# Retention layer: two of four pair sums of the absolute products move to accumulating DMAs, and PE sums four groups per phase

## The reference

```python
xf = _gn(x).reshape(B, L, E)                       # B 8, L 1024, E 256
q, k, vr = xf @ Wq.T, xf @ Wk.T * SCALING, xf @ Wv.T   # 8 heads of 32
qr, kr = theta_shift(q, sin, cos), theta_shift(k, sin, cos)
qk = einsum('bhqd,bhkd->bhqk', qr, kr) * mask
den = clip(abs(qk).sum(-1, keepdims=True), 1.0, 50000.0)
qk = qk / den
out = einsum('bhqk,bhkd->bhqd', qk, vr)
out = layernorm(out) * ln_g + ln_b                 # over the 32 of a head
x = x + gelu(out) @ Wo.T
```

## Time and profile before

| what | value |
|---|---|
| median of 3 runs | 2510.02 us (2508.24 to 2511.22) |
| profiled execution | 2510.04 us, its span 2508.2 us |
| PE busy | 2455.6 us, 98% |
| DVE busy | 1838.1 us, 73% |
| ACT busy | 1475.6 us, 59% |
| POOL busy | 885.2 us, 35% |
| retention layer, 31 of its 32 phases | 954.71 us |

### The profile page before, as it was taken

One profiled execution on the slowest core, in us unless ns is written; L12 is line 12 of the kernel. 1 busy time (PEld: TensorE's weight loads), 2 busy tenths in 40 slices (PEclk: granted clock), 3 DMA queues, 4 the chain that ended last, 5 costly groups with the idle time before them and its releaser, 6 DMA issues. The chain is left out here.

```text
span 2508.2 us, 39426 instructions
## 1 busy us (share of the span) xinstructions
PE 2455.6 (98%) x14854; PEld 1765.2 (70%) x14854; DVE 1838.1 (73%) x2789; ACT 1475.6 (59%) x2077; POOL 885.2 (35%) x627
## 2 busy tenths in 40 slices
PE   8999999999999999999999699999999999999999
PEld 4444444444444444799999588888888888888888
DVE  5888888888888888777776586666666666666665
ACT  3676666676767676566566365555555555555554
POOL 3787777777777777212112100000000000000000
PEclk9999999999999999999999899999999999999999
DMA  7232323232323233123232340000000000000000
GB/s 248 50 79 66 87 68 87 67 88 68 88 67 89 65 90 82 60 81 122 68 108 78 96 152 26 26 26 26 26 25 18 26 26 26 26 19 16 26 18 17
DMA packets 116972, 158.48 MB, mean 63 GB/s; under 512 B 16160, under 2 KB 82216, under 8 KB 116528
## 3 DMA queue, kind: packets, MB, share of 16 engines
q1 hardware_dynamic: 116256, 155.25, 21.0%
q10 hardware_dynamic: 528, 0.72, 0.1%
HBM read 71.99 MB, written 33.59 MB: 42 GB/s over the span
## 5 line engine op out<-in xcount | busy, mean ns | idle before, releaser
L579 DVE TENSOR_TENSOR l_prod<-scores,l_window 128x1024 f32<-128x1024 f32 x512 | 613.4, 1217 | 140.7 <-PE scores L438 132.7
L792 ACT ACTIVATE l_absp<-l_prod 128x1024 f32<-128x1024 f32 x512 | 540.1, 1056 | 294.9 <-DVE l_prod L579 285.0
L1887 ACT ACTIVATE e_r<-e_h,e_bn,e_rs 128x512 f32<-128x512 f32 x512 | 399.2, 780 | 484.6 <-PE e_h L1738 479.1
L438 PE MATMUL scores<-l_qst,l_kst 96*128 96x512 f32 x1024 | 379.6, 461 | 15.9 <-DVE l_prod L579 12.8
L2053 POOL TENSOR_TENSOR e_res<-e_res,e_bias 128x1024 f32<-128x1024 f32 x16 | 42.0, 2623 | 928.4 <-DMA e_res<-t_scratch 928.4
L438 PEld LDWEIGHTS scores<-l_qst,l_kst 96*128 96x128 f32 x1024 | 164.4, 189 | 274.2 <-DVE l_prod L579 134.3
L908 POOL TENSOR_TENSOR l_absp<-l_absp,l_absp 128x1024 f32<-128x1024 f32 x126 | 297.8, 2384 | 14.3 <-ACT l_absp L792 14.0
L1738 PE MATMUL e_y<-e_whi,e_h2lo 128*128 128x256 f32 x1024 | 289.8, 283 | 0.0
L1737 PE MATMUL e_y<-e_wlo,e_h2hi 128*128 128x256 f32 x1024 | 289.7, 283 | 0.0
L1736 PE MATMUL e_y<-e_whi,e_h2hi 128*128 128x256 f32 x1024 | 289.2, 282 | 0.1
L1982 DVE CAST e_h1hi<-e_r 128x512 fp32r<-128x512 f32 x256 | 111.2, 434 | 224.2 <-ACT e_r L1887 224.2
(11 more groups left out here) (266 smaller groups left out, 4760.2 us busy)
## 6 DMA issues: line engine op xcount, KB each, us to landing
l_kst<-l_hi SPq DMA_DIRECT2D x248, 64.0 KB, 2.0
l_qst<-l_hi SPq DMA_DIRECT2D x248, 64.0 KB, 2.0
l_xo<-in_x SPq DMA_DIRECT2D x32, 256.0 KB, 3.0
x_scratch<-l_xo SPq DMA_DIRECT2D x32, 256.0 KB, 2.4
l_xa<-x_scratch SPq DMA_DIRECT2D x8, 1024.0 KB, 10.4
l_xr<-x_scratch SPq DMA_DIRECT2D x8, 1024.0 KB, 8.1
t_scratch<-l_t2s SPq DMA_DIRECT2D x8, 1024.0 KB, 5.5
e_xraw<-xn2T_scratch SPq DMA_DIRECT2D x16, 512.0 KB, 3.8
```

The source lines that it names most:

```text
L438: mm = nc.tensor.matmul(sc[j][:, s, :], kst[g][0:96, h, 128 * kt:128 * kt + 128], qst[c][0:96, h, :], start=True, stop=True)
L579: nc.vector.tensor_tensor(prod[2 * (S % 2) + j][:], sc[j][:], win[:, 4 * g + 2 * j:4 * g + 2 * j + 2, w0:w0 + QC], ALU.mult).then_inc(prod ...
L792: nc.scalar.activation(absp[S % ABS][j][:], prod[2 * (S % 2) + j][:], ACT.Abs).then_inc(abs_ready, 1)
L1887: nc.scalar.activation(r[m][:], p[m][:], ACT.Relu, bias=bn_[layer][1][:, m, e:e + 1], scale=rs[layer][:, m, e:e + 1]).then_inc(done, 1)
```

## The change

- POOL issues one DMA with an accumulate operation for steps 0+1 and one for 4+5 of a phase (the last phase only 0+1): it adds the whole buffer of the first step, 1 MB, to that of the second, SBUF to SBUF. The two tiles of a buffer now lie behind each other, so that one DMA takes both. POOL waits for the second step's absolute values before it issues.
- POOL's adds of 2+3 and 6+7 stay.
- PE has four den groups per phase: (0,1) in step 4, (2,3) in step 5, (4,5) in step 0 of the next phase, (6,7) in its step 1. They were six: 0 in step 2, 1 in step 3, (2,3) in 5, 4 in 6, 5 in 7, (6,7) in step 1 of the next.
- `absolute` waits for the DMA where it writes over the first buffer of such a pair, and for the pair's den group where it writes over the second.
- In the experts' layer three semaphores are merged into others.

```diff
-    row(absp, *((f"l0_absp{s}_{j}", 4 * K) for s in range(4) for j in range(2)))
+    row(absp, *((f"l0_absp{s}", 8 * K) for s in range(4)))
...
-    def pairs(P):
+    def by_dma(P):
+        return (0, 4) if P < PHASES - 1 else (0,)
+
+    def by_pool(P):
         return (2, 6) if P < PHASES - 1 else (2,)
 
     def den_at(P):
 
         if P < PHASES - 1:
-            return {2: (0,), 3: (1,), 5: (2, 3), 6: (4,), 7: (5,), 9: (6, 7)}
-        return {2: (0,), 3: (1,), 5: (2, 3), 6: (4,), 7: (5,), 8: (6,), 9: (7,)}
+            return {4: (0, 1), 5: (2, 3), 8: (4, 5), 9: (6, 7)}
+        return {4: (0, 1), 5: (2, 3), 6: (4,), 7: (5,), 8: (6,), 9: (7,)}
...
-            if len(steps) == 2:
+            if steps[0] in dma_steps:
+                pe.wait_ge(dma_added[steps[0] % KT], 16 * (P + 1))
+            elif len(steps) == 2:
                 pe.wait_ge(pair_added, 2 * pair_of[steps[0]] + 2)
...
-                if before in pair_steps:
+                if before in dma_steps:
+                    act.wait_ge(dma_added[before % KT], 16 * (before // KT + 1))
+                elif before in pair_steps:
                     act.wait_ge(pair_added, 2 * pair_of[before] + j + 1)
                 else:
                     act.wait_ge(den_done, unit_of[before] + 1)
...
+        def dma_pair(S):
+
+            pool.wait_ge(abs_ready, 2 * (S + 1) + 2)
+            pool.dma_start(absw[(S + 1) % ABS][:].rearrange("p j s q -> p (j s q)"),
+                           absw[S % ABS][:].rearrange("p j s q -> p (j s q)"), accum_op=ALU.add).then_inc(dma_added[S % KT], 16)
...
         for P in range(PHASES):
-            if P > 0 and 6 in pairs(P - 1):
-                add_pair(KT * (P - 1) + 6, 0)
-                add_pair(KT * (P - 1) + 6, 1)
+            if P > 0:
+                pair(P - 1, 6)
+            pair(P, 0)
             if has_q(P):
                 rotate(prep_q(P), (P + 1) % 2)
                 rotated(prep_q(P))
                 low(prep_q(P), *(stacks_before_q(P) if P else (k_stacked[0], STACK)))
-            add_pair(KT * P + 2, 0)
-            add_pair(KT * P + 2, 1)
+            pair(P, 2)
             if has_kv(P):
                 rotate(prep_k(P), P % 2)
                 rotated(prep_k(P))
+            pair(P, 4)
             if P > 0:
                 scale_heads(P - 1)
...
-        biased = [sem(f"biased{c}") for c in range(2)]
+        biased = sem("biased")
```

More of the change, by code:

```diff
@@ L107, in layer0 @@
     unit_of = {s: n for n, (_, steps) in enumerate(units) for s in steps}
-    pair_steps = [KT * P + s for P in range(PHASES) for s in pairs(P)]
+    pair_steps = [KT * P + s for P in range(PHASES) for s in by_pool(P)]
+    dma_steps = [KT * P + s for P in range(PHASES) for s in by_dma(P)]
     pair_of = {s + d: n for n, s in enumerate(pair_steps) for d in range(2)}
@@ L177, in layer0 @@
     prod = [sb(f"prod{n}", [128, 2, QC]) for n in range(4)]
-    absp = [[sb(f"absp{s}_{j}", [128, 2, QC]) for j in range(2)] for s in range(ABS)]
+    absw = [sb(f"absp{s}", [128, 2, 2, QC]) for s in range(ABS)]
+    absp = [[absw[s][:, j] for j in range(2)] for s in range(ABS)]
     tA, tB = sb("tA", [128, 4, 128]), sb("tB", [128, 4, 128])
@@ L204, in layer0 @@
     pair_added = sem("pair_added")
+    dma_added = {kt: sem(f"dma_added{kt}") for kt in by_dma(0)}
     a_ready, b_ready = sems("a_ready b_ready")
@@ L909, in add_pair, with pair @@
                                     ALU.add).then_inc(pair_added, 1)
+        def dma_pair(S):
+            pool.wait_ge(abs_ready, 2 * (S + 1) + 2)
+            pool.dma_start(absw[(S + 1) % ABS][:].rearrange("p j s q -> p (j s q)"),
+                           absw[S % ABS][:].rearrange("p j s q -> p (j s q)"), accum_op=ALU.add).then_inc(dma_added[S % KT], 16)
+        def pair(P, kt):
+            if kt in by_dma(P):
+                dma_pair(KT * P + kt)
+            elif kt in by_pool(P):
+                add_pair(KT * P + kt, 0)
+                add_pair(KT * P + kt, 1)
         def scale_heads(P):
@@ L1642, in layer1_experts @@
         x_split_hi, x_split = sem("x_split_hi"), sem("x_split")
-        bn_step, bn_eps, bn_rs, bn_ready = sem("bn_step"), sem("bn_eps"), sem("bn_rs"), sem("bn_ready")
+        bn_step, bn_rs = sem("bn_step"), sem("bn_rs")
         featT_made, featT_ready, logitsT_made, logitsT_ready = (sem(n) for n in ("featT_made", "featT_ready", "logitsT_made",
@@ L1874, in _ @@
             weights_high(1)
-            act.wait_ge(bn_ready, 2)
+            act.wait_ge(bn_step, 10)
             def relu(b, u, layer, first):
@@ L1943, in _ @@
                 g, bb, be, m, v = (flat(a) for a in bn_[n])
-                nc.vector.tensor_scalar(v, v, BN_EPS, None, ALU.add).then_inc(bn_eps, 1)
+                nc.vector.tensor_scalar(v, v, BN_EPS, None, ALU.add).then_inc(bn_step, 1)
                 nc.vector.tensor_tensor(bb, bb, m, ALU.subtract).then_inc(bn_step, 1)
@@ L1960, in _ @@
                 nc.vector.tensor_tensor(flat(rs[n][:]), flat(rs[n][:]), g, ALU.mult).then_inc(bn_step, 1)
-                dve.wait_ge(bn_step, 3 + 2 * n)
+                dve.wait_ge(bn_step, 5 + 3 * n)
                 nc.vector.tensor_tensor(bb, bb, flat(rs[n][:]), ALU.mult).then_inc(bn_step, 1)
-                dve.wait_ge(bn_step, 4 + 2 * n)
-                nc.vector.tensor_tensor(bb, bb, be, ALU.add).then_inc(bn_ready, 1)
+                dve.wait_ge(bn_step, 6 + 3 * n)
+                nc.vector.tensor_tensor(bb, bb, be, ALU.add).then_inc(bn_step, 1)
             dve.wait_ge(wT_made, 1)
@@ L2003, in finish @@
                 dve.wait_ge(y_ready, U * b + NE * c + NE)
-                dve.wait_ge(biased[c], b + 1)
+                dve.wait_ge(biased, 2 * b + c + 1)
                 nc.vector.tensor_tensor(flat(res[c][:]), flat(py[c][:]), flat(res[c][:]), ALU.add).then_inc(y_read, 1)
@@ L2044, in _ @@
             for n in range(2):
-                pool.wait_ge(bn_eps, n + 1)
+                pool.wait_ge(bn_step, 2 * n + 1)
                 nc.gpsimd.tensor_tensor(flat(rs[n][:]), flat(bn_[n][4]), flat(mhalf[:]), ALU.pow).then_inc(bn_rs, 1)
@@ L2052, in add_biases @@
                     pool.wait_ge(res_in[c], 16 * (b + 1))
-                    nc.gpsimd.tensor_tensor(flat(res[c][:]), flat(res[c][:]), flat(bias[c][:]), ALU.add).then_inc(biased[c], 1)
+                    nc.gpsimd.tensor_tensor(flat(res[c][:]), flat(res[c][:]), flat(bias[c][:]), ALU.add).then_inc(biased, 1)
             add_biases(0)
```

## The result

The changed kernel takes 2536.17 us (median of 4 runs, 2531.74 to 2541.66) beside 2509.13 us of the kernel before in the same comparison: a ratio of 1.0108, 95% interval 1.0087 to 1.013. It is slower by 27 us. The profiled execution took 2536.53 us, its span is 2534.7.

What follows compares the result with a forecast made beforehand. PE was taken to bound the kernel, with DVE close behind. Waits nearly cancel PE's 55.4 us saving: -0.15 to +0.45 us per phase, mean +0.2, so +6 us over 31 phases on 2510 gives 2516 us; range 2490 to 2610.

Steps and rivals of the forecast that it cites:

- (a): ACT's abs of step 1 waits for den group (4,5), starts 1.9 us later, and delays DVE's shuffle by 1.9 us.
- PE's wait for products in step 4: Sign that the forecast holds: PE waits in step 4 for DVE's products; no size given.
- The waits for den: Sign that the forecast holds: ACT's abs waits for the den matmuls, none before, some 60 us in all.
- PE's busy time in the layer: Sign that the forecast holds: PE busy falls by some 60 us while the layer stays near 955 us.
- (b): DVE's chain from the products of step 3 through centring, clip and step 4's products runs 1.4 us late.
- (c): PE's k projection waits for the clip's bank; step 4 begins +0.4, step 5 +2.0 us; phase ends 0.15 us earlier.
- (d): Each DMA issue holds POOL 1.0 us; PE's transposes in step 7 wait 0.6 us; the phase ends 0.45 us later.
- (e): Each DMA lands in 7.5 us, 8.5 with its issue: just in time within ACT's idle time, at no cost.
- the 30 us that the prediction named as a sign of being wrong: ACT's abs waiting for a DMA over 30 us in all would mean a late transfer.
- late-DMA rival: The DMA lands in 10.4 us, the second 2.9 us too late per phase: +90, 2600 us; chance 0.28.
- The mean of +0.2 per phase: Mean change per phase between -0.15 and +0.45 us, as output projections hide part of POOL's wait; +6 us over 31 phases.
- The faster rival: ACT's delay is half absorbed: 2483 us; chance 0.18. Its sign: abs of step 1 starts less than 1 us later.

Runs made afterwards that it cites:

- experiments 1: Changed kernel with the den group (4,5) moved to the very start of step 0 of the next phase: 2513.12 us, ratio 1.0008.
- experiment 2: Kernel before the change with one added wait: ACT's abs of step 1 waits for PE's num of step 0; 2544.66 us, ratio 1.0147.
- experiment 3: Changed kernel without its DMAs (steps 0 and 4 left out of den): 2495.74 us; then with a POOL operation replacing each DMA: 2524.64 us.
- experiment 6: Changed kernel, only 4+5 by DMA, its group at the start of step 0: 2495.58 us; with first and last-but-one phases as before the change: 2492.56 us.
- experiment 4: Changed kernel without its DMAs and with the den group (4,5) at the start of step 0: 2490.63 us, ratio 0.9923.

## Why the prediction was right, point by point

The forecast was slower, 2516 in a range of 2490 to 2610; 2536 is inside it, and 20 us over the forecast. The direction and the first cause, (a), were right. The number is inside partly by luck: the forecast by itself had 2505 to 2530, and the range reached up to 2610 to take in a late DMA, while what was missing from the sum came mainly from POOL's place in other engines' chains. Of the signs named in advance, the 130 groups and PE's wait for products in step 4 came. The waits for den were 93.3 us instead of some 60, since step 5's were not foreseen, and PE's busy time in the layer fell by 25 us and not by 60.

- **(a), the wait of ACT on the new group.** As walked. The shuffle's idle time was forecast at 0.44 + 1.9 = 2.3 us and is 2.41; experiments 1 and 2 show that it reaches the time. The abs of step 1 starts 4.03 us into the phase (518.76 - 514.73), 2.03 before (505.44 - 503.41): 2.0 later, where 1.9 was forecast.
- **(b), DVE's chain.** Its size was wrong by one instruction. I took the clip for 1.95 us of work; in this phase it is 0.17 (the row at 527.02, above). But the microseconds so won did not come through: DVE waited for ACT's squares 1.23 us instead, because ACT had waited for POOL. Step 4's second products came 15.45 us into the phase (530.18 - 514.73), where 519.5 - 503.4 = 16.1 was forecast.
- **(c), PE.** Step 4 was forecast 15.8 us into the phase and is 15.7 (530.43); before, 15.4. The k projection waits for the clip's bank, as said. Step 5 begins 19.2 us in (forecast 19.8).
- **(d), POOL.** The hold was right: 0.6 us from start to start and 0.88 of record, against 1.0. That POOL's wait for abs adds nothing held in this phase too: the shuffle ends at 521.22 (520.48 + 0.74) and the issue starts at 521.55. What failed is the path. Twice in a phase an engine waits for POOL, and I walked only one of them, the transposes in step 7 (forecast 0.6 us, here 1.49). The other is ACT's high part in step 2, which had been on POOL's heels already. The q rotation begins 1.74 us after the shuffle instead of 0.86 (522.20 - 520.46, before 508.04 - 507.18), and ACT waits 1.66 us for it instead of the 0.25 of before:

```profile
512.03 0.63 ACT L777 ACTIVATE l_hi<-l_t 128x512 fp32r<-128x512 f32 x1 [0.25 <-POOL l_t L892]
```

  Behind it, DVE's variance and the second products of step 4 follow late. The longer normalisation of experiment 3 was not walked either. In experiment 3 POOL's time and place cost some 29 us, where my sum had at most 0.6 us in a phase, and 6 us in all for everything. This is the mis-sized term.
- **(e), the landing.** 7.3 us at the median, against 7.5, and in the phase walked the cover was just enough: ACT's first abs waits 3.62 us for the DMA and starts 30.4 us into the phase (545.13 - 514.73), where 30.7 (534.1 - 503.4) was the latest that should cost nothing. Over the layer ACT waited for a DMA 48.3 us in 20 waits, of which 9.3 in the first phase. That is over the 30 us that the prediction named as a sign of being wrong, and the sign was a poor one, since it counted waiting inside the cover too. With the traffic the landing is worth the 11.5 us of experiment 3, by that rough division. The late-DMA rival (+90) did not happen; the 10.4 row was of a reload from HBM. I had left the first phase out of the walk, where PE waited 8 us.
- **The mean of +0.2 per phase.** It is (978.58 - 954.71) / 31 = +0.77, and 9.3 / 25 = +0.37 in the phases at full clock; the lower clock had no term in the sum. I let the phases with an output projection hide POOL's wait. They don't all: by the windows one kind stands at 33.99 (736.20) against 32.80 before. It is the kind with the normalisation.

```profile
719.82:752.62 32.80, 32.42 (x198) 15.84 (x197) 26.78 (x29) 21.35 (x26) 25.06 (x18) 1.00 0.26 66
```
- **The faster rival.** By its own sign it was wrong: abs of step 1 starts 2.0 us later, not less than 1. DVE's 132.7 us of waiting fell to 100.2 only, so DVE did not give the room back. It was however near in another form: 4+5 alone gives 9 us, and 17 with the two edits of experiment 6.

The estimate of 6.8 us from the Trainium skill, "DMA: Bandwidth & Descriptors", section "Anatomy of one DMA - SWDGE (gpsimd) path", with both operands counted, compares with a median of 7.3 in the trace, so here the formula is a fair guide to a landing away from the start (in the first phase it took 16.8).

## What to carry to other kernels

Work taken off the busiest engine is only worth what the other engines can deliver earlier, so walk one period of every kind through every queue, with the waits that the new order of buffer releases brings; the cheapest fix may be to move the releasing instruction a few places ahead (23 us here). When an instruction is put into a helper engine's queue, list every engine that waits for anything behind it, and what will now run beside it. And try the parts of a change one by one: half of this one is faster than before, the whole is slower.

## What the runs showed that I had not expected

**The clip is short; POOL's add made it long.** In the kernel before the clip, 16 elements per partition, takes 1856 ns at the mean; in the changed kernel 638, often 0.17 us. In the kernel before, it starts 0.5 us after POOL's first add of a pair and ends when that add does. DVE's row, then POOL's:

```profile
544.20 1.95 DVE L603 TENSOR_SCALAR l_den_t<-l_den_t 128x16 f32<-128x16 f32 x1
```
```profile
543.72 4.74 POOL L908 TENSOR_TENSOR l_absp<-l_absp,l_absp 128x1024 f32<-128x1024 f32 x2
```

In experiment 2 the clip came at 558.86 and the adds began at 559.15: 0.36 us. In experiment 4 DVE was early again and the clip at 1856 ns. The Trainium skill, "SBUF — State Buffer", section "Who interferes with whom", says that a `tensor_scalar` on VectorE may take the port pair that it shares with GpSimd and that whoever comes second waits for the whole instruction. The rows agree with that rule: DVE came second, and its record ends (546.15) about when POOL's first add does (half of 4.74 after 543.72: 546.09). The rows show the coincidence in time, long beside an add and short without one; that the port is the cause is taken from the page.
